# Linear attention with an FP4 gate on one core: how the reciprocal denominators travel through DRAM

## The chip, the core and the metric

The kernel runs on one core of a Trainium2 chip. The metric is the device time of one execution in microseconds (us), as the median of several runs. The core has a matrix engine (PE, TensorE), a vector engine (DVE), an activation engine (ACT), a general engine (POOL, GpSimd) and a queue engine (SP, SyncE), which in this kernel issues every DMA. Sixteen DMA engines carry out the transfers. The engines run independently and wait for each other through counters (semaphores).

## The reference

The input `x` is [4, 2048, 256]. It is normalized to `xn`, and `xn` goes two ways: through a linear-attention layer with 16 heads of 64, and through a feed-forward gate whose operands are rounded to FP4 in blocks of 16. The result is `x + s * silu(ffn)`.

```python
xn = _layernorm(x)
q, k, v = xn @ Wq + bq, xn @ Wk + bk, xn @ Wv + bv          # (b, s, 16, 64)
Q, K = elu(q) + 1.0, elu(k) + 1.0
KV = einsum('bshd,bshm->bhdm', K, v)
Z = 1.0 / (einsum('bshd,bhd->bsh', Q, K.sum(axis=1)) + 1e-6)
o = einsum('bshd,bhdm,bsh->bshm', Q, KV, Z).reshape(b, s, 1024)
x1 = layer_norm(xn + o @ Wo + bo)
s = layer_norm(x1 + gelu(x1 @ W1 + b1) @ W2 + b2)
g = silu(fp4_linear(silu(fp4_linear(xn, w_gate)) * fp4_linear(xn, w_up), w_down))
out = x + s * g
```

`Z` is what this case is about: one reciprocal for each token and head.

## The kernel before, in words

The 8192 tokens are 64 tiles of 128, in 16 blocks of four tiles (512 tokens). A first stage (to about 425 us) normalizes, builds K and the maps `Mh`, `Ml` (KV times Wo, in a high and a low part), and quantizes the weights. The main stage then takes the blocks one after the other. All order is written out by hand: each engine has its own list of steps, and waits on counters set by the others.

The way of the denominators in block `g`, in the kernel's names:

- `den_sums(g)` on PE multiplies `ksB` with the queries `Q32`. Token tile `t` of the block gets rows 32t to 32t+31 of the PSUM piece `DN[:, 256:384]`; the first 16 of each 32 rows are the 16 heads, the columns are the tile's 128 tokens.
- `den_inverse(g)` on DVE (L1816, L1818) adds the small constant and takes the reciprocal, into the SBUF tile `dn_s` [128, 128].
- `z_out(g)` on SP (L397 to L401) stores the useful rows of `dn_s` to the DRAM scratch `z_scratch`, which holds for each block 16 heads by 512 tokens: four DMAs, one for each token tile, each of 16 rows of 512 bytes.
- `z_in(g, j)` on SP (L403 to L409), for the eight head pairs j = 0 to 7: waits for the stores (counter `zo`), and for the buffer `ZB[j % 4]` to be free (counter `zq`, set by the multiplication four pairs ago), then loads the row of head 2j into partitions 0 to 63 and that of head 2j+1 into partitions 64 to 127 of `ZB[j % 4]` [128, 512]. A load reads the same 2048-byte row 64 times.
- `z_mul(g, j)` on DVE (L1828) multiplies `Q32[:, j, :]` by `ZB[j % 4]` into a half of the PSUM bank `QH`; ACT rounds that to `RH` (L1201) and DVE subtracts for the low part `RL` (`z_lo`, L1837).
- `at_step(g, j)` on PE multiplies these by `Mh` and `Ml` into the bank `AC` (L81 to L83).

Around them, in the order of the main loop: DVE runs `z_mul(g, 0)`, `z_mul(g, 1)`, `h_lo(d - 4, 0)` (L1664, the low part of a turned tile of the gate's hidden values), then `z_lo(g, 0)`, `z_lo(g, 1)`, and so on in pairs of j. PE runs `gate_up(b, 1)`, then `turn_h(d - 4, 1)` (L831, four transposes), which needs that `h_lo(d - 4, 0)` has emptied the bank `TT`, then `at_step(g, 0)`. SP runs for each block: `z_out`, the sixteen loads of `z_in`, then the loads `xb`, `xnTh`, `xnTl` for the next block and the store of the block before.

```python
for g in range(NG):                 # SP
    z_out(g)
    for j in range(8):
        z_in(g, j)
```

Of the kernel before, what the change touches and what calls it, by code (L numbers as in the profile page):

```python
# [5 lines left out]
F32 = mybir.dt.float32  # L6
# [6 lines left out]
NG = NT // 4  # L13
# [95 lines left out]
def build(nc, src, Wq, bq, Wk, bk, Wv, bv, Wo, bo, W1, b1, W2, b2, g1, be1, g2, be2,  # L109
# [4 lines left out]
    xt_dram = nc.dram_tensor("xt_scratch", [NG, 2, 128, 1024], F32, kind="Internal").ap()  # L114
    kr_dram = nc.dram_tensor("kr_scratch", [NB, 1024], F32, kind="Internal").ap()
    ks_dram = nc.dram_tensor("ks_scratch", [NB, 128, 256], F32, kind="Internal").ap()
    z_dram = nc.dram_tensor("z_scratch", [NG, 16, 512], F32, kind="Internal").ap()

    ctx = ExitStack()
    with ctx:  # L120
        S = {n: ctx.enter_context(nc.semaphore("s_" + n)) for n in SIGNALS}
# [7 lines left out]
        def sb(name, shape, dt=F32, scope=ctx):  # L129
            return scope.enter_context(nc.sbuf_tensor(name, shape, dt))  # L130
# [50 lines left out]
        dn_s = sb("dn_s", [128, 128])  # L181
# [182 lines left out]
        def _(e):  # L364
            w = Waits(e)
# [31 lines left out]
            def z_out(g):  # L397

                w.wait_ge(S["zi"], 2 * g + 2)
                for t in range(4):  # L400
                    e.dma_start(z_dram[g, :, t * 128:(t + 1) * 128], dn_s[32 * t:32 * t + 16, :]).then_inc(S["zo"], 16)  # L401

            def z_in(g, j):  # L403

                w.wait_ge(S["zo"], 64 * (g + 1))
                w.wait_ge(S["zq"], 8 * g + j - 3)
                for s in range(2):
                    e.dma_start(ZB[j % 4][64 * s:64 * s + 64, :],  # L408
                                z_dram[g, 2 * j + s].unsqueeze(0).broadcast_to([64, 512])).then_inc(S[f"zb{j % 4}"], 16)  # L409

            def ks_row(b):

# [20 lines left out]
            for half in range(2):  # L433
                c = half * 512
# [8 lines left out]
            for i in range(NT + 2):  # L443
                if i % 4 == 2 and i // 4 + 2 < NG:
                    load_x(i // 4 + 2)
                if i in load_at:
                    n = load_at[i]
                    wt, _, _, t = W_LATER[n]
# [35 lines left out]
                if i == 8:  # L484
                    w.wait_ge(S["A_wsh"], WSH[3])
                    w.wait_ge(S["A_wsl"], WSL[3])
                    for c in range(3):
                        for t, nt, p, n, up, r in gate_up_rows(c):
                            rows = (wg, wu)[up][r:r + n * nt, :].rearrange("(t p) k -> p t k", p=n)
# [42 lines left out]
            for g in range(NG):  # L532
# [3 lines that stand above are left out]
                if g + 1 < NG:  # L536
                    load_xb(g + 1)
                    load_xn(g + 1)
                if g:
                    store(g - 1)  # L540
                if g % 4 == 3 and g + 1 < NG:
                    load_m((g + 1) // 4)
# [963 lines left out]
        def _(e):  # L1506
            w = Waits(e)
# [304 lines left out]

            def den_inverse(g):
                w.wait_ge(S["dn"], g + 1)
                w.wait_ge(S["zo"], 64 * g)
                e.tensor_scalar(dn_s[:], DN[:, 256:384], DEN_EPS, None, ALU.add).then_inc(S["zi"], 1)  # L1816
                w.wait_ge(S["zi"], 2 * g + 1)
                e.reciprocal(dn_s[:], dn_s[:]).then_inc(S["zi"], 1)  # L1818
# [117 lines left out]
            for g in range(NG):  # L1936
                a, b, c, d = 4 * g, 4 * g + 1, 4 * g + 2, 4 * g + 3
# [74 lines left out]
            q_elu(0, 7)  # L2012
            gate_mul(0, 1)
            den_inverse(0)
            gate_mul(0, 0)
            h_max(0)
# [73 lines left out]
            for g in range(1, NG - 1):  # L2090
                a, b, c, d = 4 * g, 4 * g + 1, 4 * g + 2, 4 * g + 3
                gate_mul(a, 0)
                x_round(g, 1)
                den_inverse(g)
                h_max(a)
                h_scale(a)
# [78 lines left out]
            x_round(NG - 1, 1)  # L2175
            gate_mul(NT - 4, 0)
            den_inverse(NG - 1)
            h_max(NT - 4)
            h_scale(NT - 4)
# [378 lines left out]
```

## Time and profile before

| | us |
|---|---|
| median of 3 runs (1647.0 to 1651.97) | 1648.93 |
| the profiled execution | 1644.95 |
| its span in the profile | 1643.2 |
| PE busy | 1604.9 (98%) |
| DVE busy | 1280.4 (78%) |
| ACT busy | 980.1 (60%) |
| POOL busy | 783.3 (48%) |

The profile is of one execution. "Busy" is the time in which an engine has an instruction in work; for PE it is modelled, since matrix products are pipelined. "Idle before" an instruction is charged to what released it. A DMA has three times: its issue on SP, the traffic on the sixteen DMA engines, and its landing, when its counter is complete. The chain of waits follows the work that ended last back from its end.

### The profile page before, as it was taken

The numbers are of one execution on the slowest core, as the hardware profiler recorded it, in microseconds if no ns is written. First come the engines' busy times: TensorE is split into PE (matmuls) and PEld (weight loads), VectorE is DVE, ScalarE is ACT, GpSimd is POOL, SyncE is SP. The second block draws the span as 40 slices with busy tenths as digits, with TensorE's granted clock in tenths as the row PEclk, the third lists the DMA queues.
The fourth block names the chain that finished last, engine by engine and source line by source line (L and its number), as shares of the span: only waits on it lengthen the run. The fifth ranks groups of instructions, "written<-read, shape, count | busy, mean of one in ns | idle before, by whom it ended". The sixth has DMA issues, their size and how long they took to land.

```text
span 1643.2 us, 30638 instructions
## 1 busy us (share of the span) xinstructions
PE 1604.9 (98%) x10977; PEld 1440.9 (88%) x10977; DVE 1280.4 (78%) x2485; ACT 980.1 (60%) x1770; POOL 783.3 (48%) x750
## 2 busy tenths in 40 slices
PE   7999999999899999999999999999999999999997
PEld 6878888888789998999999999989899989999897
DVE  6785664554788797888888887879788888878797
ACT  6665666655564747565665647474656656574743
POOL 4564543434242635444444536364455444363636
PEclk9999999999999999999999999999999999999999
DMA  7422323331501111133121112111121321111110
GB/s 227 136 84 86 104 78 106 103 109 57 186 15 53 52 53 52 53 111 91 47 68 53 52 53 107 53 52 53 52 60 61 104 87 58 53 52 53 52 53 26
DMA packets 92515, 123.46 MB, mean 75 GB/s; under 512 B 13503, under 2 KB 60747, under 8 KB 91342
## 3 DMA queue, kind: packets, MB, share of 16 engines
q1 hardware_dynamic: 92366, 121.51, 23.1%
q8 instruction: 88, 1.44, 0.4%
q14 instruction: 61, 0.50, 0.1%
HBM read 86.86 MB, written 34.62 MB: 74 GB/s over the span
## 4 chain that ended last, share of the span: by engine, by line
PE 68%; DVE 13%; DMA 7%; issue 5%; SPq 3%; ACT 3%; POOL 2%; DVEq 0%; POOLq 0%; ACTq 0%
PE QH L81 11%; PE QH L82 11%; PE QH L83 10%; PE AC L81 5%; PE AC L82 4%; PE AC L83 4%; DMA zb<-z_scratch 4%; PE GU L81 4%; PE GU L83 4%; PE GU L82 4%; DVE QH L1828 2%; PE TT L831 2%; DVE rl L1837 2%; SPq L408 2%; DMA z_scratch<-dn_s 1%
## 5 line engine op out<-in xcount | busy, mean ns | idle before, releaser
L2309 POOL TENSOR_TENSOR hb<-hb,rs_h 128x704 f32<-128x704 f32 x64 | 89.0, 1391 | 206.3 <-DVE rs_h L1680 206.3
L1248 ACT ACTIVATE hb<-GU 128x352 f32<-128x352 f32 x128 | 59.2, 463 | 214.3 <-PE GU L83 214.3
L1201 ACT ACTIVATE rh<-QH 128x512 fp32r<-128x512 f32 x256 | 151.2, 598 | 58.2 <-DVE QH L1828 53.2
L81 PE MATMUL GU<-wgh,xqh 128*128 128x352 f32 x512 | 169.8, 332 | 3.1 <-DVE hb L1673 3.1
L2315 POOL TENSOR_TENSOR hb<-hb,sn_h 128x64 f32<-128x64 f32 x64 | 18.8, 293 | 319.5 <-DVE hb L1685 319.5
L83 PE MATMUL GU<-wgh,xql 128*128 128x352 f32 x512 | 165.0, 322 | 0.0
L82 PE MATMUL GU<-wgl,xqh 128*128 128x352 f32 x512 | 164.9, 322 | 0.0
L1843 DVE TENSOR_TENSOR rl<-QH,rh 128x512 fp32r<-128x512 f32 x128 | 86.0, 682 | 85.8 <-ACT rh L1201 83.7
L81 PE MATMUL AC<-Mh,rh 128*128 128x256 f32 x512 | 145.9, 285 | 1.4 <-ACT rh L1201 0.6
L81 PE MATMUL AC<-w2h,rh 128*128 128x256 f32 x512 | 145.7, 285 | 0.0
L82 PE MATMUL AC<-Ml,rh 128*128 128x256 f32 x512 | 142.4, 278 | 0.0
L82 PE MATMUL AC<-w2l,rh 128*128 128x256 f32 x512 | 142.3, 278 | 0.0
L83 PE MATMUL AC<-Mh,rl 128*128 128x256 f32 x512 | 142.3, 278 | 0.0
L83 PE MATMUL AC<-w2h,rl 128*128 128x256 f32 x512 | 142.2, 278 | 0.0
L1564 DVE SCALAR_TENSOR_TENSOR u<-ex,QH 128x512 f32<-128x512 f32 x128 | 84.8, 681 | 51.2 <-ACT ex L1135 50.9
L1214 ACT ACTIVATE QH<-QH,cols 128x512 f32<-128x512 f32 x128 | 84.7, 661 | 48.4 <-PE QH L83 44.0
L1135 ACT ACTIVATE ex<-QH,neg 128x512 f32<-128x512 f32 x128 | 86.1, 686 | 45.9 <-PE QH L83 44.5
L81 PE MATMUL QH<-wkh,xth 128*128 128x512 f32 x256 | 105.0, 410 | 2.0 <-DVE xtl L1547 1.1
L81 PE MATMUL QH<-xTh,w1h 128*128 128x512 f32 x256 | 104.7, 409 | 0.6 <-DVE rl L1843 0.6
L1658 DVE SCALAR_TENSOR_TENSOR Q<-QH,eg 128x512 f32<-128x512 f32 x128 | 87.7, 686 | 21.7 <-ACT QH L1198 20.5
L1196 ACT ACTIVATE eg<-QH 128x512 f32<-128x512 f32 x128 | 76.4, 597 | 45.2 <-PE QH L83 44.9
L81 PE MATMUL QH<-xnTh,wqh 128*128 128x512 f32 x256 | 102.0, 398 | 0.0
(234 smaller groups left out, 5586.0 us busy)
## 6 DMA issues: line engine op xcount, KB each, us to landing
zb<-z_scratch SPq DMA_DIRECT2D x256, 128.0 KB, 3.0
xa<-in_L_attn_src SPq DMA_DIRECT2D x16, 512.0 KB, 4.2
xt_scratch<-xth SPq DMA_DIRECT2D x32, 256.0 KB, 2.7
xt_scratch<-xtl SPq DMA_DIRECT2D x32, 256.0 KB, 3.0
xb<-in_L_attn_src SPq DMA_DIRECT2D x16, 512.0 KB, 4.2
xnTh<-xt_scratch SPq DMA_DIRECT2D x32, 256.0 KB, 4.8
xnTl<-xt_scratch SPq DMA_DIRECT2D x32, 256.0 KB, 5.6
out<-x SPq DMA_DIRECT2D x15, 512.0 KB, 6.6
```

The source lines that it names most:

```text
L81: e.matmul(outp, lh, rh, start=start, stop=False, skip_group_check=check)
L82: e.matmul(outp, lh, rl, start=False, stop=False, skip_group_check=check)
L83: return e.matmul(outp, ll, rh, start=False, stop=stop, skip_group_check=check)
L1135: e.activation(Ex[:, c:c + 512], QH[:, c:c + 512], ACT.Exp, bias=neg1[:, 0:1]).then_inc(S["A_e"], 1)
L1196: e.activation(EG[j % 2][:], q_bank(j), ACT.Relu).then_inc(S["qr"], 1)
L1201: e.activation(RH[j % 4][:], src, ACT.Copy).then_inc(S[sem], 1)
L1214: e.activation(q_bank(j), q_bank(j), ACT.Gelu, bias=b1c[:, j:j + 1]).then_inc(S["ge"], 1)
L1248: e.activation(HB[i % 3][:, hf * HALF:(hf + 1) * HALF], gu_bank(i, hf)[:, 0:HALF], ACT.Tanh, scale=0.5).then_inc(S["th"], 1)
L1564: e.scalar_tensor_tensor(U[i % 2][:, c:c + 512], Ex[:, c:c + 512], 1.0, QH[:, c:c + 512], ALU.min, ALU.max).then_inc(S["A_K"], 1)
L1658: e.scalar_tensor_tensor(Q32[:, j, :], bank, 1.0, r[:], ALU.min, ALU.add).then_inc(S["Q"], 1)
L1843: e.tensor_tensor(RL[j % 4][:], QH[:, (j % 2) * 512:(j % 2 + 1) * 512], f(RH[j % 4][:]), ALU.subtract).then_inc(S["gel"], 1)
L2309: e.tensor_tensor(hb, hb, spread(rs_h[i % 2][:], 44), ALU.mult).then_inc(S["hin"], 1)
```

## The change

The scratch `z_scratch` becomes 128 by 128 for each block, the shape of `dn_s`. `z_out` stores the whole tile as it stands, all 128 rows of 512 bytes, by one DMA; the 64 rows that are no heads go along. The counter `zo` therefore grows by 16 a block and not by 64. `z_in` keeps its two loads for each j; the row of a head now lies in four pieces of 512 bytes, 32 rows apart, and each of the 64 target partitions gathers the four. `den_inverse` waits on the new count.

```diff
-    z_dram = nc.dram_tensor("z_scratch", [NG, 16, 512], F32, kind="Internal").ap()
+    z_dram = nc.dram_tensor("z_scratch", [NG, 128, 128], F32, kind="Internal").ap()
@@ z_out(g)
                 w.wait_ge(S["zi"], 2 * g + 2)
-                for t in range(4):
-                    e.dma_start(z_dram[g, :, t * 128:(t + 1) * 128], dn_s[32 * t:32 * t + 16, :]).then_inc(S["zo"], 16)
+                e.dma_start(z_dram[g], dn_s[:]).then_inc(S["zo"], 16)
@@ z_in(g, j)
-                w.wait_ge(S["zo"], 64 * (g + 1))
+                w.wait_ge(S["zo"], 16 * (g + 1))
                 w.wait_ge(S["zq"], 8 * g + j - 3)
+                rows = z_dram[g].rearrange("(t h) c -> h t c", t=4)
                 for s in range(2):
                     e.dma_start(ZB[j % 4][64 * s:64 * s + 64, :],
-                                z_dram[g, 2 * j + s].unsqueeze(0).broadcast_to([64, 512])).then_inc(S[f"zb{j % 4}"], 16)
+                                rows[2 * j + s].unsqueeze(0).broadcast_to([64, 4, 128])).then_inc(S[f"zb{j % 4}"], 16)
@@ den_inverse(g)
-                w.wait_ge(S["zo"], 64 * g)
+                w.wait_ge(S["zo"], 16 * g)
```

No instruction of PE, DVE, ACT or POOL changes place. On SP the four stores of a block become one; the rest keeps its order.

## Rows read from the trace of the kernel before

**Rows 1.** The page: busy time of each engine, its share of the span, instructions.

```profile
PE 1604.9 (98%) x10977; PEld 1440.9 (88%) x10977; DVE 1280.4 (78%) x2485; ACT 980.1 (60%) x1770; POOL 783.3 (48%) x750
```

**Rows 2.** Window of block 4: length, busy times, TensorE clock, DMA share, GB/s.

```profile
734.68:810.11 75.43, 74.72 (x559) 69.25 (x558) 63.43 (x125) 45.49 (x82) 36.68 (x33) 1.00 0.19 57
```

**Rows 3.** Waits, 433 to 1643 us: who for whom, us in total, times, longest.

```profile
DVE QH L1828 <- DMA zb<-z_scratch: 14.9, 28, 1.6
...
PE TT L831 <- DVE hql L1664: 8.7, 14, 1.7
```

**Rows 4.** PE timeline: start, us, line, operation [idle before, releaser]: blocks 0 and 4, three others.

```profile
442.27 0.35 PE L81 MATMUL AC<-Mh,rh 128*128 128x256 f32 x1 [0.57 <-ACT rh L1201]
...
743.51 0.63 PE L831 MATMUL TT<-ident,hb 128*128 128x128 f32 x4 [0.44 <-DVE hql L1664]
...
1047.42 0.63 PE L831 MATMUL TT<-ident,hb 128*128 128x128 f32 x4 [1.66 <-DVE hql L1664]
...
1199.36 0.63 PE L831 MATMUL TT<-ident,hb 128*128 128x128 f32 x4 [1.13 <-DVE hql L1664]
...
1578.00 0.63 PE L831 MATMUL TT<-ident,hb 128*128 128x128 f32 x4 [1.12 <-DVE hql L1664]
```

**Rows 5.** Chain of waits in block 4: start, us, what.

```profile
734.68 0.32 SPq L401
...
735.97 1.45 DMA z_scratch<-dn_s
...
737.43 0.45 SPq L408
...
737.93 3.16 DMA zb<-z_scratch
```

**Rows 6.** SP timeline in block 4, the z loads, then the loads after them.

```profile
737.43 10.12 SPq L408 DMA_DIRECT2D zb<-z_scratch  x16
...
773.73 1.02 SPq L386 DMA_DIRECT2D xnTh<-xt_scratch  x2
```

**Rows 7.** DVE timeline in block 4: the products that read the z loads.

```profile
741.11 0.70 DVE L1828 TENSOR_TENSOR QH<-Q,zb 128x512 f32<-128x512 f32 x1 [0.28 <-DMA zb<-z_scratch]
742.34 0.70 DVE L1828 TENSOR_TENSOR QH<-Q,zb 128x512 f32<-128x512 f32 x1 [0.53 <-DMA zb<-z_scratch]
...
750.47 1.29 DVE L1828 TENSOR_TENSOR QH<-Q,zb 128x512 f32<-128x512 f32 x2
...
752.66 1.28 DVE L1837 TENSOR_TENSOR rl<-QH,rh 128x512 fp32r<-128x512 f32 x2
```

**Rows 8.** PE timeline in block 4: the first product of `at_step(g, 6)`.

```profile
754.89 0.29 PE L81 MATMUL AC<-Mh,rh 128*128 128x256 f32 x1
```

**Rows 9.** The page's DMA issues: operation, count, KB each, median us to landing.

```profile
zb<-z_scratch SPq DMA_DIRECT2D x256, 128.0 KB, 3.0
...
m_scratch<-mh SPq DMA_DIRECT2D x16, 256.0 KB, 2.4
...
z_scratch<-dn_s SPq DMA_DIRECT2D x64, 8.0 KB, 1.4
...
out<-x SPq DMA_DIRECT2D x4, 128.0 KB, 1.7
```

**Rows 10.** DMA traffic, 742.5 to 748 us (z loads): packets, MB, share of 16 engines.

```profile
DMA packets 671, 1.10 MB, mean 200 GB/s; under 512 B 134, under 2 KB 134, under 8 KB 671
...
q1 hardware_dynamic: 671, 1.10, 65.1%
```

**Rows 11.** The same, 549 to 558 us: loads of 1 KB rows and an output store.

```profile
q1 hardware_dynamic: 2116, 2.07, 68.6%
```

**Rows 12.** The same, 735 to 737.4 us: the four z stores alone.

```profile
DMA packets 128, 0.03 MB, mean 14 GB/s; under 512 B 64, under 2 KB 128, under 8 KB 128
...
q1 hardware_dynamic: 128, 0.03, 6.9%
```

**Rows 13.** The same, 1007.5 to 1012.5 us: loads of 8 KB rows, mostly.

```profile
DMA packets 796, 2.13 MB, mean 426 GB/s; under 512 B 44, under 2 KB 606, under 8 KB 606
```

## The prediction

> **What bounds the kernel now.** I read the page's busy times first. PE is at work for 98% of the span and DVE for 78% [rows 1], and a window of block 4 shows the same in small: of 75.43 us PE is busy 74.72, its clock at full speed [rows 2]. So only what removes idle time of PE can move the time, and only little of that is left. Next I read the waits of the main stage [rows 3]. DVE stands idle 14.9 us, 28 times, for the z loads. That is DVE's idle time and not the kernel's. The row under it matters: PE waits 8.7 us, 14 times, for `hql`, which is written by `h_lo`, the DVE instruction queued right behind `z_mul(g, 0)` and `z_mul(g, 1)`. The PE timeline shows the places [rows 4]: once a block, 0.44 us in block 4, and in three blocks 1.66, 1.13 and 1.12 us. Thirteen of the 14 are this place, 8.3 us together (the other, 0.4 us, lies later in block 0); in block 0 the z loads delay the first product of `at_step` instead, by 0.57 us. All other waits of PE from block 1 on are about 0.2 us each, but for a few.
>
> The chain of waits says what makes `z_mul` late [rows 5]. The reciprocals are ready, the first store is issued at 734.68, the fourth at 735.97, and it lands 1.45 us later. Only then, at 737.43, does the first load go, and the load issued at 737.93 lands 3.16 us after that. So the z way is 2.75 us of store and 3.7 us of load before the first product, and DVE is short of it by 0.28 us at `z_mul(g, 0)` and 0.53 us at `z_mul(g, 1)` [rows 7].
>
> **Part 1: four stores become one.** From the first issue to the first load it takes 737.43 - 734.68 = 2.75 us now. With one store it takes that store's landing alone. Bounds for 64 KB in 128 rows: 1.4 us, the landing of an 8 KB z store, and 2.4 us, that of a 256 KB store of `mh`. Nearest is the final store of 128 KB in 128 rows, 1.7 us [rows 9]. Between 1.4 at 8 KB and 1.7 at 128 KB, 64 KB gives 1.55 us. The loads then start 2.75 - 1.55 = 1.2 us earlier (0.35 to 1.35 by the bounds). The 64 rows that nobody reads cost traffic on idle DMA engines, since the four stores keep them 6.9% busy [rows 12]. On SP three issues of 0.42 us go; nothing is queued behind them but the loads themselves.
>
> **Part 2: the loads come in 512-byte pieces.** Each load had 64 pieces of 2 KB, four for each of the 16 DMA engines; it now has 256 of 512 bytes, sixteen for each. What a piece costs now: 65.1% of 5.5 us times 16 engines is 57.3 us for 537 pieces and 134 semaphore packets [rows 10], 107 ns a 2 KB piece, semaphores included, so 4 x 107 = 0.43 us a load. What does a 512-byte piece cost? No load in the trace has it. Below: a quarter of 107, that is 27 ns. The z stores' own 512-byte pieces: 6.9% of 2.4 us times 16 is 2.65 us for 64 pieces, 41 ns each with one semaphore packet to each piece [rows 12], which is high for our case. Above: the 1 KB pieces of the next loads and the output store, 68.6% of 9 us times 16 over 2116, 47 ns [rows 11]. I take 31 to 41 ns.
>
> The pace then depends on two numbers. SP issues a z load every 10.12 / 16 = 0.63 us [rows 6]. Sixteen pieces of 41 ns take 0.66 us, so at 40 ns a piece the DMA engines become as slow as SP; at 31 ns they have 0.5 us of work and SP stays the pace. `z_mul(g, 1)` waits for the fourth load. It starts 742.34 - 737.43 = 4.9 us after the first load's issue; the landing without the moving of data is 3.0 - 0.43 = 2.57 us. At 41 ns the fourth load lands 4 x 0.66 + 2.57 = 5.2 us after it, 0.3 us later than now; at 31 ns 3 x 0.63 + 0.5 + 2.57 = 5.0, 0.1 us later. I take 0.2 us. Issues themselves I leave at 0.6 us: two `xnTh` loads of 256 pieces each take 1.02 us for both [rows 6], so more pieces do not slow an issue in that row.
>
> The Trainium skill has a rule against this part ("DMA: Bandwidth & Descriptors", section "Why small descriptors are slow (HBM only)"): each packet carries about three extra cycles beside one cycle per 32 bytes. By it four pieces of 512 bytes would cost 76 cycles where one of 2 KB costs 67, 13% more, an estimate of 30 ns a piece; the sum would then lose 0.1 us of load time and not 0.2. No run here shows a load of such pieces.
>
> **Part 3: what the earlier loads are worth.** Net, the z data come 1.2 - 0.2 = 1.0 us earlier. DVE has the slack for that: at `z_mul(g, 0)` and `z_mul(g, 1)` together it gives back 0.81 us in block 4, where PE lacks only 0.44. The PE wait goes wherever it is at most 1.0 us and shrinks by 1.0 us in the three longer ones: 8.3 - (0.66 + 0.13 + 0.12) + 0.57 in block 0 = 8.0 us. What is late next is the start of `at_step(g, 0)`, whose `z_lo` moves with the same DVE queue, and then PE's own work. Nothing gives the gain back that I can find: everything behind it (the first norm, the turning of `x1`, the next projections) hangs on `at_step`, and moves with it.
>
> The profiled execution would go from 1644.95 to 1637.0 us, and the median, 4 us above it, from 1648.93 to about **1641 us**.
>
> **Rivals.**
>
> A. *The forecast*: 1641, on its own 1635 to 1644.5. The upper end is a store that lands after 2.4 us, which leaves 0.35 us in each block and takes some 4.3 us off. The lower end has all the waits of this place gone and, since the median is 4 us above the profile, some longer ones that the profile did not catch.
>
> B. *The loads give back what the store gains.* At 53 ns a piece a load takes 0.85 us; the fourth lands 4 x 0.85 + 2.57 = 6.0 us after the first issue, 1.1 us later than now, and the 1.2 us are used up. Time 1645 to 1650, middle 1648. For it: the z loads pay 107 ns for 2 KB where the traffic of 8 KB rows runs at 426 GB/s, 77 ns for each 2 KB [rows 13], so a repeated row does carry some 30 ns extra for each piece. Against it: 1 KB pieces take 47 ns with all they carry. The same time would come of stray slow landings: if the 1.66 us block is an accident of the DMA queue and not of having four stores, it may happen again.
>
> C. *The loads become the bound, slower.* If those 30 ns are paid by each piece whatever its size, a 512-byte piece costs 30 plus a quarter of 77 to 41: 50 to 71 ns. The place that breaks is the end of the row: `z_mul(g, 7)`, now at 751.1 us (the second of its two), 13.7 us after the first issue; add the 1.2 us gained and the 0.95 us between the last `z_lo` (to 753.94) and `at_step(g, 6)` (754.89) [rows 7, 8], and the sixteenth load may land 15.8 us after the first issue. That is 16 loads of 0.83 us, 52 ns a piece. At 60 ns they take 16 x 0.96 + 2.57 = 17.9 us, and PE is 2.1 us later than now in each of 16 blocks, the old wait of this place included: 1649 + 34 = 1683. Against it speaks again the 47 ns of whole 1 KB pieces, which leaves no room for a fixed 30 in a piece of half the size unless a repeated row is special.
>
> D. *The pieces are not cut as the text says* (the engines write 2 KB and read in some other size). Then the loads cost what they cost now, the z data come 1.2 us earlier and the gain is 8.3 to 9 us: within A's range.
>
> **How the numbers follow.** A with D 0.57, B 0.26, C 0.17. What a measurement of this kernel can tell from no change is about 0.3%, 5 us. Of A, 0.03 gains less than that, and goes to no change; B has 0.01 on the slow side. So faster 0.54, same 0.28, slower 0.18. C is left out of the range, which takes in A and B: 1635 to 1652.
>
> **What would show each step.** Part 1: one z store a block, landing after about 1.55 us, and 1.6 us from its issue to the first load where 2.75 stood. Part 2: 256 packets a load of 31 to 41 ns, DMA share in the z loads up from 65% to 75 to 100%, landing 3.1 to 3.3 us, issues still 0.6 us apart. Part 3: the row of DVE waiting for `zb` falls from 14.9 us to under 5, and PE's row for `hql` from 8.7 us to about 1. It would be wrong if the z loads take over 0.8 us each of the DMA engines, if their issue on SP slows to 0.8 us, or if PE's wait moves to `at_step` or the x1 turns at its old size.

## The result

The changed kernel takes 1689.47 us (median of 4 runs, 1687.5 to 1692.1), the kernel before 1649.51 us beside it: a ratio of 1.0243, with a 95% interval of [1.0225, 1.0261]. It is 40 us slower, where the forecast was 8 us faster.

| | before | after |
|---|---|---|
| the profiled execution, us | 1644.95 | 1689.61 |
| its span, us | 1643.2 | 1687.8 |
| PE busy, us | 1604.9 | 1618.1 |
| PE idle (span less busy), us | 38.3 | 69.7 |
| z store to landing, us | 1.4 | 1.5 |
| z load to landing, us | 3.0 | 4.8 |
| mean granted TensorE clock | 0.999 | 0.993 |

The span grew by 44.6 us: 31.4 us more idle PE and 13.2 us more "busy" PE. The page of the changed kernel, busy times and the z loads' row of its DMA issues, beside [rows 1, 9]:

```profile
PE 1618.1 (96%) x10977; PEld 1450.1 (86%) x10977; DVE 1283.3 (76%) x2485; ACT 980.1 (58%) x1770; POOL 785.6 (47%) x750
...
zb<-z_scratch SPq DMA_DIRECT2D x256, 128.0 KB, 4.8
```

The waits from 433 us to the end, as in [rows 3]: who waited for whom, us in total, times, longest:

```profile
DVE QH L1828 <- DMA zb<-z_scratch: 50.7, 60, 2.8
...
PE TT L831 <- DVE hql L1664: 23.8, 16, 2.7
PE GU L81 <- DVE hb L1673: 12.5, 11, 3.2
...
PE AC L81 <- DVE rl L1837: 5.2, 7, 1.3
```

DVE's wait for the loads went from 14.9 to 50.7 us. PE's wait for `hql` went from 8.7 to 23.8 us, and two more appear: for `hb` (12.5 us, 3.1 before) and for `rl` (5.2 us, 0.5 before), both written by DVE instructions that stand behind the products of the z loads.

The chain of waits in block 4, which answers to [rows 5]: start, us, what.

```profile
753.52 1.52 DMA z_scratch<-dn_s
...
755.05 0.58 SPq L408
...
755.68 5.55 DMA zb<-z_scratch
```

The store part is as forecast: 1.53 us from the issue of the store to the first load, where 2.75 stood and 1.6 was expected. The load that `z_mul(g, 0)` waits for lands 5.55 us after its issue, 3.16 before. The loss begins there, and DVE's timeline shows it at `z_mul(g, 0)`, which waited 0.28 us before:

```profile
761.25 0.70 DVE L1828 TENSOR_TENSOR QH<-Q,zb 128x512 f32<-128x512 f32 x1 [1.44 <-DMA zb<-z_scratch]
```

The decisive view is the DMA traffic in the 6 us from a block's first load (block 4 in each kernel; 40 slices of 0.15 us, GB/s in each, then packets and the share of the 16 engines). Before:

```profile
GB/s 0 0 0 0 0 0 0 0 68 150 191 164 164 96 137 232 178 287 287 260 232 150 109 109 178 300 178 287 260 219 178 123 218 232 123 150 246 260 205 164
```

After:

```profile
GB/s 0 0 0 0 0 0 0 0 0 3 51 34 14 48 48 48 41 41 48 44 41 41 44 65 99 140 106 126 154 171 171 178 222 253 266 263 266 239 202 171
DMA packets 1124, 0.55 MB, mean 91 GB/s; under 512 B 59, under 2 KB 1124, under 8 KB 1124
...
q1 hardware_dynamic: 1124, 0.55, 36.6%
```

From 1.95 to 3.45 us after the first issue the traffic stands at 41 to 48 GB/s, then it climbs. Yet the engines are little busy. Over the 6 us, 36.6% times 16 engines is 35 us for 1065 pieces, 33 ns a piece. In the slow stretch alone, 756.4 to 758.4 us, it is 151 pieces and a share of 19.4%:

```profile
q1 hardware_dynamic: 151, 0.08, 19.4%
```

These are fewer than the 256 pieces of one load, and no semaphore packet, by which an engine ends its share of a load, is among them: the slow stretch falls within the first load. A piece costs an engine what I had forecast, and the loads are late all the same.

### The profile page after: what moved, and what is told of

Its sections match the earlier page's. It is cut to its first block, busy times and chain, and to the rows that moved or that the text cites. A ratio compares the mean times of both kernels' runs of the same rounds, so it can differ in the third digit from the quotient of the medians.

```text
span 1687.8 us, 30590 instructions
## 1 busy us (share of the span) xinstructions
PE 1618.1 (96%) x10977; PEld 1450.1 (86%) x10977; DVE 1283.3 (76%) x2485; ACT 980.1 (58%) x1770; POOL 785.6 (47%) x750
## 3 DMA queue, kind: packets, MB, share of 16 engines
q8 instruction: 88, 1.44, 0.4%
## 4 chain that ended last, share of the span: by engine, by line
PE 68%; DVE 12%; DMA 11%; issue 3%; SPq 3%; ACT 2%; POOL 1%; DVEq 0%; POOLq 0%; ACTq 0%
PE QH L81 11%; PE QH L82 10%; PE QH L83 10%; DMA zb<-z_scratch 9%; PE AC L81 5%; PE AC L82 5%; PE AC L83 5%; PE GU L81 4%; PE GU L83 4%; PE GU L82 4%; SPq L408 3%; PE TT L831 2%; DMA z_scratch<-dn_s 1%; DVE QH L1828 1%; DVE rl L1837 1%
## 5 line engine op out<-in xcount | busy, mean ns | idle before, releaser
L81 PE MATMUL GU<-wgh,xqh 128*128 128x352 f32 x512 | 171.2, 334 | 12.5 <-DVE hb L1673 12.5
L1828 DVE TENSOR_TENSOR QH<-Q,zb 128x512 f32<-128x512 f32 x128 | 87.7, 696 | 51.3 <-DMA zb<-z_scratch 50.7
L81 PEld LDWEIGHTS GU<-wgh,xqh 128*128 128x128 f32 x512 | 96.6, 189 | 17.2 <-issue 11.3
L81 PEld LDWEIGHTS AC<-Mh,rh 128*128 128x128 f32 x512 | 99.2, 194 | 12.1 <-ACT rh L1201 7.6
```

Source lines behind the costliest of these rows:

```text
L81: e.matmul(outp, lh, rh, start=start, stop=False, skip_group_check=check)
L1828: e.tensor_tensor(QH[:, (j % 2) * 512:(j % 2 + 1) * 512], Q32[:, j, :], ZB[j % 4][:], ALU.mult).then_inc(S["zq"], 1)
```

## The experiments

Two theories to begin with. **Count**: a load of 256 pieces is slow because it has four times the pieces (cutting them, or handling them one after the other). **Place**: it is slow because 64 partitions read the same few short stretches of DRAM, and these share a place in memory whose rate is the limit. The times of the kernel before beside the four groups of runs are 1648.7, 1647.26, 1649.88 and 1648.13 us.

**One store, whole rows.** The change's store with loads of 2 KB.

```diff
-                rows = z_dram[g].rearrange("(t h) c -> h t c", t=4)
+                rows = z_dram[g].rearrange("(r t) c -> r (t c)", t=4)
-                    ... rows[2 * j + s].unsqueeze(0).broadcast_to([64, 4, 128])
+                    ... rows[2 * j + s].unsqueeze(0).broadcast_to([64, 512])
```

> The one store of the change, with loads of 2 KB rows as before; a load takes one contiguous 2048-byte row of the new scratch, so it brings other denominators than the head's own (the values are not the reference's, the work is). If the store part is worth what the forecast gave it and the whole loss is in the loads, the time is about 1641 us, z loads land 3.0 us after issue, and PE's wait for hql is about 1 us in all. If the store part is itself to blame (the 64 KB store disturbs what follows), the time is over 1650 us and the loads land later than 3.0 us.

Measured: 1631.06 us, ratio 0.9888 [0.9874, 0.9903]; loads land after 3.0 us. The store part is a gain, and twice the forecast one: 17.6 us in the medians, 14.5 us in the spans (1643.2 to 1628.7). Page and waits of this run:

```profile
PE 1598.9 (98%) x10977; PEld 1440.8 (88%) x10977; DVE 1276.8 (78%) x2485; ACT 976.0 (60%) x1770; POOL 788.5 (48%) x750
```

```profile
DVE QH L1828 <- DMA zb<-z_scratch: 2.4, 5, 0.9
PE TT L831 <- DVE hql L1664: 1.1, 3, 0.4
```

PE's idle time fell from 38.3 to 29.8 us, by 8.5 us, which is the 8.0 us of the forecast. The other 6.0 us left its *busy* time. Here is how, on PE's timeline in block 4, around `turn_h(d - 4, 1)`. Before:

```profile
742.75 0.32 PE L83 MATMUL GU<-wgh,xql 128*128 128x352 f32 x1
...
744.07 0.36 PE L81 MATMUL AC<-Mh,rh 128*128 128x256 f32 x1
```

With one store and whole rows:

```profile
740.99 0.33 PE L83 MATMUL GU<-wgh,xql 128*128 128x352 f32 x1
741.15 0.60 PE L831 MATMUL TT<-ident,hb 128*128 128x128 f32 x4
741.50 0.37 PE L81 MATMUL AC<-Mh,rh 128*128 128x256 f32 x1
```

From the last gate product to the first of `at_step` it is 1.32 us in the one and 0.51 us in the other. The wait costs 0.81 us where the row says 0.44 [rows 4], since a product's modelled end covers the start of the idle time, and the transposes after a wait take longer to hand on. That difference of 0.37 us is about the same for every wait, long or short, so it can't be multiplied by 16: three blocks of this run still wait. Summed over the 16 blocks, the distance between these two products fell from 22.65 to 10.18 us, by 12.5 us, of which PE's idle rows show 8.3. So 4.1 us of the 6.0 are found here; the rest of the gain of 14.5 us, 2.0 us in all, lies elsewhere and was not followed up.

**The pieces alone, close together.** Four stores, pieces of 512 bytes at a step of 1 KB.

```diff
-    z_dram ... [NG, 16, 512]
+    z_dram ... [NG, 16, 4, 256]
-                    e.dma_start(z_dram[g, :, t * 128:(t + 1) * 128], ...
+                    e.dma_start(z_dram[g, :, t, 0:128], ...
-                                z_dram[g, 2 * j + s].unsqueeze(0).broadcast_to([64, 512])
+                                z_dram[g, 2 * j + s, :, 0:128].unsqueeze(0).broadcast_to([64, 4, 128])
```

> The four stores as before, but into a scratch whose row is four pieces of 512 bytes at a step of 1 KB, and loads in four pieces of 512 bytes. If the number of pieces in a load sets its time, loads land after 4.8 us as in the changed kernel and the time is the changed kernel's plus the store gain that is missing: about 1697 us. If the place of the pieces matters (in the changed kernel they lie 16 KB apart), the loads land sooner, between 3.0 and 4.8 us, and the time is under 1690 us.

Measured: 1657.19 us, ratio 1.0045 [1.0031, 1.006], landing 3.2 us. The same number of pieces as in the changed kernel, each still read by 64 partitions, and the landing is 0.2 us longer than with whole rows, not 1.8.

**Two pieces of 1 KB**, `[NG, 16, 2, 512]`, half of each kilobyte pair used.

> A dose between: four stores as before, into a scratch whose row is two pieces of 1 KB at a step of 2 KB, and loads of two pieces of 1 KB. If landing grows with the number of pieces, it is 3.0 us plus a third of the growth, about 3.6 us, and the time lies between 1650 and 1665 us. If only the far apart pieces of the changed kernel are slow, it lands after 3.0 us and the time is 1649 us.

Measured: 1653.51 us, ratio 1.0026 [1.0015, 1.0036], landing 3.1 us. So cutting a row costs 0.1 us of landing for two pieces and 0.2 us for four, in time 5 and 8.5 us, and this is all that the count explains.

**The same pieces, not shared.** The changed kernel with a row of its own for each partition.

```diff
-                                rows[2 * j + s].unsqueeze(0).broadcast_to([64, 4, 128])
+                                xt_dram[g, j % 2, 64 * s:64 * s + 64, :].rearrange("p (t c) -> p t c", t=4)[:, :, 0:128]
```

> The changed kernel with z loads of the same number and size of pieces (256 pieces of 512 bytes), but each target partition reads four pieces of a row of its own, out of the xt scratch, where all 64 partitions read the same four pieces before (so the products are multiplied by other values than the reference's). If the repeated reading of one short address range is what is slow, the loads land after about 3 us and the time is about 1641 us. If the number of pieces sets the time, they land after 4.8 us and the time stays at about 1689 us.

Measured: 1632.99 us, ratio 0.9899 [0.988, 0.9919], landing 3.0 us. Its traffic from the first load in block 4:

```profile
GB/s 0 0 0 0 0 0 0 0 20 65 109 259 318 157 68 154 314 287 79 215 321 198 82 79 143 270 297 154 150 287 273 120 92 212 318 246 106 232 294 164
```

There is no plateau at 48 GB/s. 256 pieces of 512 bytes are no burden here, nor were they much of one in the run before the last: the count theory falls. This run changes two things, though. The pieces are not shared, and they lie 1 KB apart, in rows 4 KB apart. Unshared pieces 16 KB apart were not run, so what sharing alone adds at that distance stays open.

**Whole rows, not shared**: `xt_dram[g, j % 2, 64 * s:64 * s + 64, 0:512]`.

> One store, and loads of 2 KB in which each partition reads a row of its own out of the xt scratch (values not the reference's). Compared with the one store and the repeated 2 KB rows (1631 us, landing 3.0 us): if repeating a row costs 2 KB loads anything, they land sooner here, about 2.7 us, and the time is 1627 to 1631 us; if repetition alone costs nothing, landing 3.0 us and the same time within 3 us.

Measured: 1630.4 us, ratio 0.988 [0.9842, 0.9919], landing 2.8 us. Sharing a whole row costs 0.2 us of landing (3.0 against 2.8) and, within the spread of two runs, no time. The engine time of a 2 KB piece is the same too: from 740 to 746 us the engines are 62.5% busy with 567 pieces, 106 ns each, where the shared rows paid 107 ns.

**One piece, read four times**: all four pieces are the head's first.

```diff
-                                rows[2 * j + s].unsqueeze(0).broadcast_to([64, 4, 128])
+                                z_dram[g, 2 * j + s].unsqueeze(0).unsqueeze(0).broadcast_to([64, 4, 128])
```

> The changed kernel, but each load reads one and the same 512-byte piece four times for every partition instead of four pieces 16 KB apart (the factors of tiles 1 to 3 are then tile 0's, so the values are not the reference's). If the pieces 16 KB apart are slow because each read must turn from one memory page of a bank to another, one piece read over and over is fast: loads land after 3.0 to 3.3 us and the time is about 1635 us. If they are slow because all requests go to one place whose rate is the limit, this is as slow as the changed kernel: 4.8 us, about 1689 us or more.

Measured: 1694.01 us, ratio 1.0266 [1.0224, 1.0307], landing 4.9 us. Its traffic in block 4:

```profile
GB/s 0 0 0 0 0 0 0 0 0 41 48 44 44 44 44 44 34 44 48 38 44 55 85 113 123 161 184 106 113 116 120 184 232 256 311 260 256 225 195 215
```

The plateau, most of it at 44 to 48 GB/s with single slices down to 34, is the changed kernel's, and here every request of a load goes to one and the same 512 bytes. Turning between distant pieces is not what costs, then. The four pieces 16 KB apart are served much as if they were one.

The changed kernel's own blocks bear this out, since they run the same instructions and, of the z loads, only the addresses differ. The first load of a block lands after 4.5 us or more in twelve blocks, but after 3.9, 3.3, 4.1 and 3.3 us in blocks 2, 6, 10 and 14; the same four blocks have the fastest first loads in the run with four stores and pieces 16 KB apart, below. With one piece read four times it is 4.6 to 5.0 us in all sixteen.

**The loads of the change, without its store.** Four stores into the same places, `[NG, 4, 32, 128]`.

> The loads of the changed kernel alone: four stores as before, each of 16 rows, into the same places of the scratch that the one store fills in the changed kernel, and the same loads of four pieces 16 KB apart. If the place of the pieces alone makes the loads slow, they land after 4.8 us, and the time is the changed kernel's plus the store gain that is missing, 1689 + 16 to 20 = about 1705 us. If it takes the one large store before them to make them slow, they land after 3.2 us and the time is about 1657 us.

Measured: 1709.33 us, ratio 1.037 [1.0345, 1.0395], landing 4.7 us. The loads need no large store before them to be slow: their layout alone costs 62 us, and with the one store the time is 20 us less. That these 20 us are near the 17.6 us of the one store by itself is in part chance, since TensorE's clock comes in. The mean granted clock is 0.981 here and 0.993 in the changed kernel, which is up to 20 us by itself (0.019 of 1707.6 us less 0.007 of 1687.8 us).

**How far apart is far?** With one store, only the length of a scratch row was changed. That sets the distance of a head's four pieces, and also the distance from one head's row to the next. With four stores, both were set by the layout.

```diff
-    z_dram ... [NG, 128, 128]
+    z_dram ... [NG, 128, 144]         # 256, 160, 136, 132 in the others
-                e.dma_start(z_dram[g], dn_s[:]).then_inc(S["zo"], 16)
+                e.dma_start(z_dram[g, :, 0:128], dn_s[:]).then_inc(S["zo"], 16)
```

> The changed kernel with one thing else: a row of the scratch takes 576 bytes of which 512 are used, so that the four pieces of a head's row lie 18 KB apart and not 16 KB. One store of 128 rows and loads of 4 x 512-byte pieces as in the changed kernel. If pieces that lie 16 KB apart (a shared memory channel) are what is slow, loads land after 3.0 to 3.4 us and the time is 1632 to 1640 us, faster than both kernels. If any four pieces far apart from each other are slow, they land after 4.8 us and the time is about 1689 us.

> The same with rows of 1024 bytes of which 512 are used: the pieces of a head's row lie 32 KB apart, again a multiple of 16 KB. If the multiple of 16 KB matters, the loads land after 4.8 us or later and the time is about 1689 us or above. If padding as such helps (neighbouring rows no longer adjacent), it is as fast as rows of 576 bytes, under 1645 us.

> As the run with rows of 576 bytes, with rows of 640 bytes: the four pieces of a head's row lie 20 KB apart, which is 4 KB more than a multiple of 16 KB where 576 bytes gave 2 KB more. If only distances that are multiples of 8 KB are slow, loads land after 3.3 us or sooner and the time is 1632 to 1640 us. If a step of 4 KB is slow too, they land later than 3.6 us and the time is over 1645 us.

> The changed kernel with rows of 544 bytes: the four pieces of a head's row lie 17 KB apart, 1 KB over a multiple of 16 KB. If the distance counts modulo a power of two, this behaves as pieces 1 KB apart do: loads land after 3.2 us, and with the one store the time is 1634 to 1640 us. If it does not, anything between 3.2 and 4.8 us is possible, and the time is over 1645 us.

> The same with rows of 528 bytes: 16.5 KB apart, half a KB over a multiple of 16 KB. By the modulo reading the four pieces then cover one stretch of 2 KB, as the contiguous row of the kernel before does: landing 3.0 to 3.3 us, time 1632 to 1640 us. If closeness to 16 KB is what counts, it is slow, over 4 us and over 1660 us.

> A dose of the distance: four stores, the scratch 4 x 16 rows of 512 bytes, so that the pieces of a head's row lie 8 KB apart. If 8 KB apart still shares what 16 KB apart shares, loads land after 4.8 us and the time is about 1705 us; if half of it, between 3.2 and 4.8 us; if it shares nothing, 3.2 us and about 1657 us, as with pieces 1 KB apart.

> Four stores of 16 rows and loads of four 512-byte pieces 4 KB apart. By the modulo reading this is like 20 KB apart: landing about 3.7 us, and with four stores a time of 1665 to 1675 us. If multiples of 8 KB alone are slow, it lands after 3.2 us and the time is 1657 us as with pieces 1 KB apart.

| pieces of a head apart | stores | load lands after, us (median) | first load of a block, us (median) | time, us | ratio to before |
|---|---|---|---|---|---|
| 16 KB (the change) | 1 | 4.8 | 4.7 | 1689.47 | 1.0243 |
| 32 KB (rows of 1024 bytes) | 1 | 4.5 | 4.3 | 1682.85 | 1.0209 |
| 20 KB (rows of 640) | 1 | 3.7 | 3.3 | 1646.93 | 0.9989 [0.9976, 1.0002] |
| 18 KB (rows of 576) | 1 | 3.3 | 3.0 | 1639.22 | 0.9943 [0.9922, 0.9964] |
| 17 KB (rows of 544) | 1 | 3.4 | 3.0 | 1640.61 | 0.9958 [0.9942, 0.9975] |
| 16.5 KB (rows of 528) | 1 | 4.3 | 3.0 | 1664.04 | 1.0096 |
| 16 KB | 4 | 4.7 | 4.6 | 1709.33 | 1.037 |
| 8 KB | 4 | 5.0 | 4.7 | 1716.04 | 1.0411 |
| 4 KB, heads 16 KB apart | 4 | 9.5 | 3.8 | 1873.72 | 1.1368 |
| 1 KB, heads 4 KB apart | 4 | 3.2 | 3.0 | 1657.19 | 1.0045 |

Multiples of 8 KB are slow throughout, 1, 17 and 18 KB land nearly as soon as a whole row (though they cost 8 to 9 us of time against it), and 20 KB lies between. With 576 bytes a row, the change's own two parts make a kernel that is 8 us faster than the kernel before and 50 us faster than the changed one.

Two rows of the table spoil the simple rule that only the remainder by 16 KB counts: rows of 528 bytes should have been fast and were not, and 4 KB should have been like 20 KB and is by far the worst. The first load of each block, which has no other load before it, says more. With rows of 528 bytes it lands after 3.0 us, as the rule had it, and with 4 KB after 3.8, which is not far from the 3.3 of 20 KB. It is the loads behind it that come late: the fourth after 4.4 and 7.2 us. This points to two things that count: where the pieces of one load lie, and where those of the neighbouring heads lie, whose loads are under way at the same time. In the run with 4 KB the heads' rows lie 16 KB apart, so that all sixteen loads go to places a multiple of 4 KB apart. For rows of 528 bytes this is an explanation that no run tested. That such rows begin off a multiple of 64 bytes does not explain it: heads 4 and 8 begin on one and land after 4.4 us, and rows of 544 bytes begin off one for every odd head and are fast. The traffic of the run with 4 KB from a block's first load, 40 slices of 0.5 us:

```profile
GB/s 36 89 80 41 74 75 80 85 79 90 291 287 118 109 93 79 56 103 80 113 47 79 89 81 26 0 0 0 0 0 0 0 0 0 0 33 0 0 0 0
```

With several loads under way, most slices stay between 74 and 113 GB/s, but for one stretch of 1 us at 287 to 291. In the changed kernel the heads lie next to each other, and traffic climbs from 48 to 266 GB/s as loads of other heads join. Both fit a place in memory with a rate of its own, that many requests can meet at. That is the reading which the runs leave standing, not something that a trace shows directly, and which bits of an address choose the place stays open.

**Another way to the same gain.** The layout of before, with two of the four stores issued from ACT's queue.

```diff
-                for t in range(4):
+                for t in range(2):                      # and range(2, 4) on ACT, after gate_tanh(a, 0); in block 0 after gate_tanh(1, 0)
                     e.dma_start(z_dram[g, :, t * 128:(t + 1) * 128], ...
```

> The kernel before, its scratch and its 2 KB loads, with two of the four stores of a block issued by ACT's queue beside the other two on SP's, so that no head's row is cut in pieces and two issues of 0.42 us leave the way. If the store part is worth its time on the path and nothing else, the first load goes 0.8 us earlier and the time is 1634 to 1640 us. If a store queued on ACT disturbs ACT's work or lands later, the time is 1645 us or more.

Measured: 1642.56 us, ratio 0.9955 [0.9943, 0.9968], a gain of 7 us and somewhat under the expected one. The issue on the path fell as said: first load 1.98 us after the first store, where 2.75 stood. PE's timeline shows what is missing, in block 0:

```profile
446.07 0.55 PE L81 MATMUL AC<-Mh,rh 128*128 128x256 f32 x1 [4.23 <-ACT rh L1206]
```

The wait there is 4.23 us, where 0.57 us stood, and the granted clock is 0.50 from 446 to 451 us. There ACT comes to its two stores only at 438.02, behind a gate function that waits for PE, 4.6 us after SP stored its own at 433.4. The place in ACT's list was wrong for this one block.

## Why the prediction was wrong

**What bounds the kernel**: right. The waits named there are where the time went, and the first place of loss is PE's wait for `hql`.

**Part 1, the store**: the time on the way was right (1.53 us measured, 1.6 forecast), its worth was mis-sized: 8.0 us forecast, 14.5 us measured in the spans. The step "the PE wait goes wherever it is at most 1.0 us", summed over PE's idle rows to 8.0 us, gives the idle time well (8.5 us in the run with one store and whole rows) but takes a row's idle time for the whole price of the wait. In block 4 the price is nearly twice that, 0.81 for 0.44 us, and over the 16 blocks it is 12.5 us for 8.3.

**Part 2, the loads**: the cost of a piece was right (31 to 41 ns forecast, 33 measured), and so was the forecast that SP issues them nearly as before. The step that failed is "the landing without the moving of data is 3.0 - 0.43 = 2.57 us", carried over unchanged, so that only the engines' busy time could grow. The first load of block 4 lands 5.2 us after its issue, 2.8 before. Its 16 pieces of 33 ns on each engine are 0.53 us of work, so the part that was to stay at 2.57 us is 4.7 us. In those 2.1 us more the engines are mostly idle. That the pieces wait for memory is inferred, from the runs that changed little but where the reads go: one piece four times is as slow, and pieces 17 and 18 KB apart are fast. In the forecast the place of the pieces was no quantity at all, and neither was it that 64 readers share them. The 107 ns of a shared 2 KB piece against 77 ns of a 2 KB share of an 8 KB row [rows 10, 13] looks like a hint, and was read in rivals B and C as the price of a repeated row. It is neither: with a row of its own for each partition a 2 KB piece takes 106 ns.

**The rivals**: C named 1683 us and 1689.47 was measured, but by another mechanism. C had the DMA engines as the bound, at 50 to 71 ns a piece and the break at the last load of a row. Measured are 33 ns, engines 36.6% busy over the first 6 us, and the break already at the first loads: `z_mul(g, 0)` waits in block 4 for 1.44 us. That its time came near is luck. The 47 ns of 1 KB pieces, held against C, were sound evidence against its mechanism. D fell too, the pieces are 512 bytes: 1065 of them in 0.55 MB.

**The Trainium skill's rule** ("DMA: Bandwidth & Descriptors", section "Why small descriptors are slow (HBM only)"), by which a load in pieces of 512 bytes was worked out to be 13% dearer, an estimate of 30 ns a piece, agrees with the engine time: 29 ns a piece where the pieces are not shared (54.1% of 6 us times 16 engines over 1781 pieces), 33 ns in the changed kernel. It says nothing of the 1.8 us of landing, which come with the place of the pieces.

**What would show it**: the signs of the good case failed. The landing was to be 3.1 to 3.3 us and was 4.8, DVE's wait was to fall under 5 us and was 50.7, and PE's wait for `hql` was to fall to about 1 us and was 23.8. The DMA share was to rise from 65% to 75 or more, and was 63.3% over the same stretch of block 4 (760.12 to 765.62 us). Of the signs of error none came as written. A load took 0.53 us of the engines' time and not over 0.8, its issue stayed at 0.6 us, and PE's wait did not move to `at_step`: it grew where it stood, and 5.2 us more came at `at_step` beside it. A slow load on idle engines was not among the cases that I had thought of.

## What to carry to other kernels

Where many partitions read the same data from DRAM, its layout is part of the cost: a row in one contiguous 2 KB stretch landed after 3.0 us here, in four pieces 1, 17 or 18 KB apart after 3.2 to 3.4 us, and in four pieces 8, 16 or 32 KB apart after 4.5 to 5.0 us, with the same bytes. To keep off multiples of 8 KB was not enough, since the rows of loads under way together count too (4.3 us with rows of 528 bytes, 9.5 us with pieces 4 KB and heads 16 KB apart): try a few row lengths and measure. Read the landing of a transfer apart from the busy share of the DMA engines, since a load can be late on idle engines. And one short wait of PE can cost more than its idle row: take the distance between the work before and the work behind it, and compare that with a block that doesn't wait.

## What the runs showed of the hardware

A load that reads one 512-byte piece 256 times, or four pieces 16 KB apart 64 times each, moved at some 41 to 48 GB/s for its first 1.5 us, on engines that were 19.4% busy, where a load of unshared pieces of the same size, 1 KB apart, reached 318 GB/s. With all loads of a block in places 4 KB and 16 KB apart, most of the traffic stayed between 74 and 113 GB/s.

The longer waits also cost clock. In block 1 of the changed kernel PE is at work for 3.06 of 5 us, and the granted clock in the 5 us after that is 0.70, a mean of the two levels, 2.4 GHz and 1.2 GHz (windows: length, busy times, clock, DMA share, GB/s):

```profile
525.00:530.00 5.00, 3.06 (x20) 2.67 (x19) 3.11 (x6) 2.06 (x5) 0.72 (x2) 0.96 0.54 151
530.00:535.00 5.00, 5.00 (x34) 5.00 (x33) 4.30 (x7) 2.19 (x6) 0.00 (x0) 0.70 0.56 150
```

In windows of 10 us from 425 to 1625 us the clock is below full in five, in blocks 0, 1, 9 and 15, at 0.66, 0.83, 0.96, 0.87 and 0.84, which makes 8.4 us of clock lost (the sum of ten times one less the clock), the larger part of the 13.2 us by which PE's busy time grew. In the kernel before no such window was below full. Another 1.7 us of clock went in the first stage, 0.83 in each of the two 5 us windows from 45 to 55 us, and has nothing to do with the z loads: the run with one store and whole rows lost the same there. Across the runs the mean granted clock mostly falls as PE waits longer for `hql`: 0.998 with 1.1 us of waits (one store, whole rows), 0.993 with 23.8 (the change), 0.981 with 40.6 (16 KB, four stores), 0.959 with 75.1 (4 KB). It is no fixed price, since the run with one piece read four times kept 0.996 with 27.7 us. The forecast, and rival C, had no term for it.
